# Attention in a hybrid kernel: from one head over all queries to chunks of 512 queries and groups of four heads, with the keys of all heads kept in SBUF

## What is computed

```python
    # 16 heads of 8 dimensions, L = 2048 tokens
    scores = jnp.einsum('bhqd,bhkd->bhqk', q, k) * scale
    scores = scores + alibi_bias(H, L)[None]      # -inf where the key is later than the query
    attn = jax.nn.softmax(scores, axis=-1)
    ctx = jnp.einsum('bhqk,bhkd->bhqd', attn, v)
    ctx = ctx.transpose(0, 2, 1, 3).reshape(B, L, E)
    return jnp.einsum('ble,fe->blf', ctx, w_out)
```

## Time and profile before

| | us |
|---|---|
| median of 3 runs (2050.13 to 2059.32) | 2055.5 |
| the profiled execution, its own time | 2052.21 |
| its span, first to last instruction | 2050.4 |
| what lies around the span | 1.8 |
| attention a0, first instruction to last addition to x | 514.8 to 993.7 |
| attention a1, the same | 1517.2 to 1990.7 |

### The profile page before, as it was taken

How to read it: one execution, slowest core, us unless ns; L and a number is a source line. 1 busy time by engine, 2 the same in 40 slices (tenths; PEclk the granted TensorE clock), 3 DMA queues, 4 the chain that set the end, 5 groups by cost and what they waited for, 6 DMA issues and landing times. The chain is left out here.

```text
span 2050.4 us, 47996 instructions
## 1 busy us (share of the span) xinstructions
PE 1835.4 (90%) x18588; PEld 979.6 (48%) x18588; DVE 1588.0 (77%) x3383; ACT 1175.0 (57%) x2361; POOL 553.9 (27%) x520
## 2 busy tenths in 40 slices
PE   6888888999799999998799978888769999999967
PEld 2444454444255555554544424444543555555454
DVE  6799965666889999983555568999668999999545
ACT  4676623222278888886222256765343888888815
POOL 3799930000200000000100037999230000000022
PEclk9899998999699999999799988999886999999969
DMA  5343300411302332211031022444012233322200
GB/s 158 102 139 123 134 1 1 83 52 31 110 25 54 52 52 57 52 26 22 2 83 52 31 62 95 127 123 118 1 58 66 51 56 58 59 57 42 30 5 21
DMA packets 68271, 126.88 MB, mean 62 GB/s; under 512 B 20919, under 2 KB 30676, under 8 KB 66572
## 3 DMA queue, kind: packets, MB, share of 16 engines
q1 hardware_dynamic: 67628, 123.27, 23.8%
q10 hardware_dynamic: 416, 0.54, 0.1%
HBM read 105.15 MB, written 16.84 MB: 59 GB/s over the span
## 5 line engine op out<-in xcount | busy, mean ns | idle before, releaser
L1757 ACT ACTIVATE a_probs<-a_ps_k 128x512 f32<-128x512 f32 (+3 forms) x1280 | 598.8, 546 | 225.0 <-PE a_ps_k L1671 128.7
L1653 PE MATMUL a_ps_q<-a_k_op,a_q_op 84*32 84x512 bf16 (+7 forms) x5120 | 537.1, 366 | 24.2 <-DMA a_k_op<-a_k_parts 9.0
L1817 DVE TENSOR_REDUCE a_maxes<-a_ps_q 128x1 f32<-128x512 f32 x768 | 504.2, 686 | 66.4 <-PE a_ps_q L1653 63.7
L1667 PE MATMUL a_ps_k<-a_q_op,a_k_op 87*32 87x512 bf16 (+7 forms) x5120 | 518.7, 353 | 2.4 <-ACT a_probs L1757 0.6
L1689 PE MATMUL a_ps_o<-a_probs,a_vh 128*32 128x512 f32 (+3 forms) x2752 | 318.4, 508 | 1.3 <-ACT a_probs L1757 0.8
L1653 PEld LDWEIGHTS a_ps_q<-a_k_op,a_q_op 72*32 72x32 bf16 (+1 forms) x5120 | 187.6, 97 | 170.4 <-DVE a_maxes L1817 69.0
L1814 DVE CUSTOM_DVE_ANT_0 a_ps_q<-a_ps_q,all_c_mask_q 128x128 f32<-128x128 f32 (+3 forms) x512 | 248.3, 496 | 5.4 <-PE a_ps_q L1653 4.3
L1667 PEld LDWEIGHTS a_ps_k<-a_q_op,a_k_op 75*32 75x32 bf16 (+1 forms) x5120 | 185.9, 96 | 135.6 <-ACT a_probs L1757 85.3
L1088 ACT ACTIVATE e_silu<-e_psg,all_me_b 128x512 f32<-128x512 f32 x128 | 87.7, 687 | 229.1 <-PE e_psg L1020 229.0
L1897 POOL CAST a_max_parts<-a_neg_max 128x16 bf16<-128x16 f32 x32 | 6.3, 196 | 750.5 <-DVE a_neg_max L1822 750.5
L1171 DVE SCALAR_TENSOR_TENSOR e_mid<-e_psv,all_me_b,e_silu 128x512 f32<-128x512 f32 x128 | 95.8, 750 | 128.8 <-PE e_psv L1022 125.0
(11 more groups left out here) (295 smaller groups left out, 2590.6 us busy)
## 6 DMA issues: line engine op xcount, KB each, us to landing
m0st_c_rows<-m_bc_rows SPq DMA_DIRECT2D x32, 512.0 KB
e_w_rows<-e_comb SPq DMA_DIRECT2D x64, 256.0 KB, 3.3
m1st_c_rows<-m_bc_rows SPq DMA_DIRECT2D x32, 512.0 KB
a_q_op<-a_q_parts SPq DMA_DIRECT2D x30, 288.0 KB
a_k_op<-a_k_parts SPq DMA_DIRECT2D x30, 288.0 KB
a_outputs<-a_o_sb SPq DMA_DIRECT2D x480, 18.0 KB
m0st_b_rows<-m_bc_rows SPq DMA_DIRECT2D x32, 256.0 KB
m1st_b_rows<-m_bc_rows SPq DMA_DIRECT2D x32, 256.0 KB
```

The source lines that it names most:

```text
L1653: last = pe.matmul(ps_q[32 * r:32 * r + 32, use % QB, 0:width], q_op[h % SLOT][0:NR, part(t, r)], k_op[h % SLOT][0:NR, kc * CH:kc * CH + w ...
L1667: last = pe.matmul(ps_k[32 * r:32 * r + 32, b % KB, 0:width], k_op[h % SLOT][:, part(j, r)], q_op[h % SLOT][:, c * CH + first:c * CH + fir ...
L1757: act.activation(probs[:, n % PSLOT, 0:width], ps_k[:, b % KB, 0:width], ACT.Exp).then_inc(exp_done, 1)
L1817: dve.tensor_reduce(found, bank, AX.X, ALU.max).then_inc(q_read, 1)
```

## The change

The work is regrouped. There are 16 steps: for each chunk of 512 queries, four groups of four heads. A step holds four heads' items of one chunk of queries, so steps have 16, 32, 48 and 64 items, four steps of each.

- The keys of all heads lie in SBUF, one operand buffer of 16 heads by 512 keys for each chunk (`k_op[c]`), loaded once. Chunk 0 is loaded by group of four heads on SP, chunks 1 to 3 on ACT's queue, each in one DMA of 72 rows by 8192 elements, once the chunk's parts are stored, and all of it stands in ACT's program ahead of the first exponential. Before it projects its third chunk, ACT waits until the first chunk's parts are stored, and so on (the parts have two buffers in place of four).
- The query operands have four slots by step (72 rows by 4 heads by 512).
- The order of the weights is changed so that dimensions come first and heads second; a chunk's rows then lie one behind the other in DRAM.
- The first form runs one step and 14 items ahead. Where the next step is longer, it issues items of the first form faster than one to one (2, 1.5 and 1.33 to one in steps 3, 7 and 11). In the last step there is none.
- The outputs of chunk c are loaded back, added, inverted, divided and projected while chunk c + 1 runs; `spread` and `output` use the banks of the first form. For c = 0 to 2 the addition of the partials is wholly on POOL. Only chunk 3 is left for the end.
- The values keep 9 columns a head (8 and a one) for all heads, in place of four slots of 32; POOL no longer copies them head by head. The banks are set to zero once.
- Stores take two heads in a DMA; the sums lie on 64 partitions by 128 in place of 128 by 64 (SB = 4).

```diff
+        k_last = m.sb("k_op3", [NR_MAX, HEADS * CH], BF16)
+        k_op = [m.sb(f"k_op{c}", [NR_MAX, HEADS * CH], BF16) for c in range(NC - 1)] + [k_last]
+        q_op = [m.sb(f"q_op{s}", [NR_MAX, HG * CH], BF16) for s in range(SLOT)]
+        vh = m.sb("vh", [P, NT * HEADS, DH + 1])
...
+        def position(b):
+            s, i = k_items[b][0], b - begin[k_items[b][0]]
+            after = size[s + 1] if s < LAST else size[s]
+            return min(begin[s + 1] + LEAD + -(-(i + 1) * after // size[s]), POSITIONS)
+        def event(c, n):
+            return position(begin[GROUPS * (c + 1)] + n)
+        prepare_at = {event(c, 24): c for c in range(NC - 1)}
+        spread_at = {event(c, 34): c for c in range(NC - 1)}
+        output_at = {event(c, 42): c for c in range(NC - 1)}
+        stats_at = {event(c, 46): c for c in range(NC - 1)}
+        normalise_at = {event(c, 60): c for c in range(NC - 1)}
...
+        def load_k(eng, c, first, n, sem):
+            rows = k_dram[c:c + 1, :, :, first:first + n, :].rearrange("o d b h t -> o (d b) (h t)")
+            eng.dma_start(k_op[c][0:PAIRS, first * CH:(first + n) * CH],
+                          rows.broadcast_to([SPL, SPL * DH, n * CH])).then_inc(sem, 16)
...
@@ PE
-            stream(turn, item, 0, NQ + LEAD)
+            first_forms(0, begin[1] + LEAD)
...
+            for b in range(NI):
+                if b + KB < NI:
+                    scores(b + KB)
+                first_forms(done, position(b))
+                done = position(b)
+                if b % 4 == 3:
+                    times_v(b - 3)
+            spread(NC - 1)
+            output(NC - 1)
@@ ACT
             for c in range(NC):
+                if c >= 2:
+                    act.wait_ge(stored[c - 2], STORED)
                 for o in range(2):
...
+            for c in range(1, NC):
+                act.wait_ge(stored[c], STORED)
+                if c == NC - 1:
+                    load_k_rows(act, c)
+                load_k(act, c, 0, HEADS, k_loaded[c])
             for b in range(AHEAD):
                 exps(b)
@@ POOL
+            for s in range(STEPS):
+                c = chunk_of(s) - 1
+                if c > 0 and s % GROUPS == 1:
+                    add_partials(c)
+                split_maxima(s)
+                if c >= 0 and s % GROUPS == 1:
+                    if c == 0:
+                        add_partials(c)
+                    ahead.power(pool, c)
@@ SP
+                for i, ready in enumerate((first_part, second_part, third_part)):
                     sp.wait_ge(ready[1], c + 1)
-                sp.dma_start(k_dram[:, :, :, chunk(c)].rearrange("h d s t -> (h d) s t"),
-                             parts[1][:, :, c, :]).then_inc(stored[c], 16)
+                    sp.dma_start(k_dram[c, :, i, :, :], parts[1][:, i, c % 2, :]).then_inc(stored[c], 16)
...
+            for c in range(NC - 1):
+                load_k_rows(sp, c)
+            store_parts(0)
+            sp.wait_ge(stored[0], STORED)
+            for i in range(GROUPS):
+                load_q(i)
+                load_k(sp, 0, HG * i, HG, k_first[i])
+                if i + 1 < NC:
+                    store_parts(i + 1)
             load_maxima(0)
```

More of the change, by code:

```diff
@@ L53 @@
 LORA = 32
-SB = P // HEADS
+SB = 4
 class Memory:
@@ L1583, in attention @@
[L1583 to L1594, removed]
+        QLOADS = 16 * (2 if alibi else 1)
+        KROWS = 16 * (2 if alibi else 1)
+        STORED = 16 * 2 * SPL
@@ L1656, in item, with spread @@
                 last.then_inc(q_ready, 1)
-            def scores(b):
-                h, n = divmod(b, NK)
-                c, j, first, width = k_items[n]
-                if n == 0:
-                    pe.wait_ge(max_loaded[h % SLOT], 16 * (h // SLOT + 1))
+            def spread(c):
+                use = spread_use[c]
+                pe.wait_ge(inverted, c + 1)
+                bank_free(use)
+                for j in range(SB):
+                    last = pe.matmul(ps_q[:, use % QB, j * JT:(j + 1) * JT], g["sel_head"][:, j, :], inv[:, :], start=True, stop=True)
+                last.then_inc(q_ready, 1)
@@ new lines, in output, with first_forms @@
+            def output(c):
+                use = output_use[c]
+                pe.wait_ge(q_read, spread_use[c] + 1)
+                bank_free(use)
+                for j in range(TPC):
+                    last = pe.matmul(ps_q[:, use % QB, tile(j)], total[:, tile(j)], w["wo"][:, :], start=True, stop=True)
+                last.then_inc(q_ready, 1)
+            def first_forms(begins, stops):
+                for p in range(begins, stops):
+                    if p in turn_at:
+                        turn(turn_at[p])
+                    if p in spread_at:
+                        spread(spread_at[p])
+                    if p in output_at:
+                        output(output_at[p])
+                    if p < NI:
+                        item(p)
@@ L1690, in times_v @@
                               start=j < 4, stop=j >= TPC * c, skip_group_check=True).then_inc(pv_done, 1)
[L1692 to L1695, removed]
-                for j in range(SB):
-                    last = pe.matmul(ps_s[:, j * JT:(j + 1) * JT], g["sel_head"][:, j, :], inv[:, :], start=True, stop=True)
-                last.then_inc(spread_ready, 1)
-            def output(c):
-                pe.wait_ge(normed, c + 1)
-                if c >= 2:
-                    pe.wait_ge(added, c - 1)
-                for j in range(TPC):
-                    last = pe.matmul(ps_y[:, c % 2, tile(j)], total[:, c % 2, tile(j)], w["wo"][:, :], start=True, stop=True)
-                last.then_inc(y_ready, 1)
@@ new lines, in _ @@
+            for c in range(NC - 1):
[7 more added lines that the diff above has]
+                    store_parts(i + 1)
+            load_maxima(0)
+            sp.wait_ge(stored[NC - 1], STORED)
+            for s in range(STEPS):
+                c = chunk_of(s)
+                if s:
+                    store(s - 1, 1)
+                if s and s + SLOT - 1 < STEPS:
+                    load_q(s + SLOT - 1)
+                if c == 0:
+                    load_maxima(s + 1)
+                if c and s % GROUPS == 0:
+                    load_outputs(c - 1, s - 1, 0, HEADS)
+                if c == NC - 1 and s % GROUPS:
+                    load_outputs(c, s - 1, head(s - 1, 0), HG)
+                if s < LAST:
+                    store(s, 0)
+                    if c:
+                        load_maxima(s + 1)
@@ L2023 @@
+            for hh in range(HG):
+                sp.wait_ge(o_read, HG * LAST + hh + 1)
+                if hh < HG - 1:
+                    move_sums(sp, hh)
+                move_outputs(sp, hh)
 MAMBA = ["in_T", "conv_w", "conv_b", "x_T", "dt_T", "dt_b", "a_log", "d", "out_T"]
```

542 lines of the change are left out of this document (256 added, 286 removed).

## The result

The changed kernel takes 2194.6 us, median of 4 runs (2193.1 to 2200.9), against 2055.0 of the kernel before on the same chip: ratio 1.0686, 95% interval 1.0654 to 1.0718. Slower, as forecast, but by 139.6 us instead of 59, and outside the range. The profiled execution has a span of 2191.0 us, 140.6 more than before.

A forecast was written before the change was run, and what follows sets the result against it. The kernel before was taken as PE bound with poor ends. First score 25.0 us later and the rest 4.6 longer made 29.6 us an attention, 59 for two: 2114 us, range 2050 to 2142.

The forecast's parts named there:

- Three engines, ACT's program as a gate: Beginning: each chunk's keys take 15.1 us on three engines at 78 GB/s; no exponential precedes the third load in ACT's program.
- The maxima land at 584 to 596 ... I take 587: Beginning: step 0's maxima wait behind group 3's 30 packets (4.7 us), plus up to 10 us for their own 16.
- The pitch of the steps: Stream: PE sets 8.95, 18.8, 29.6 and 40.3 us a step by chunk; DVE bounds steps 3, 7, 11 at 16.7, 26.3, 35.9.
- the prediction's own sign of being wrong: Stream: a step of chunk 3 that differs from 40.3 us by over 1 us would show the forecast wrong.
- the term for the clock: Stream: 4.3 us added because the second form began with 8 us at clock 0.53, which stays so.
- The spreads and outputs: 7.0: Stream: spreads and outputs of three chunks, 1.16 us each on PE, add 7.0 us to a stream PE bounds.
- DVE's own work for them fits into its slack, nearly; POOL's three additions have 15 us: Stream: DVE's 4.9 us a chunk for projections nearly fits its slack of 2 to 4 us a step.
- The end: After the last copy: only chunk 3 is left, a chain of 15 us in place of 21.3.
- 1: Key loads do no harm: first score at 554, 11 us earlier, 6.4 gained an attention, 2043 us; chance 0.16.
- 2: Key loads harm partly: first score at about 570 + 3, 8 later, 4.6 longer, 2080 us; chance 0.14.
- 4: Nothing measurable: earlier start and longer stream cancel, first score at 560, 2055 us; chance 0.08.
- Rival 3: PE stays at 1.2 GHz through chunk 0's steps: 27 us an attention on top, up to 2165; chance 0.10.

The follow-up runs named there:

- Experiment 2: Changed kernel with ACT's loads of keys of chunks 1 to 3 issued as four loads of four heads, rows of 4 KB instead of 16 KB: 2180.6 us.
- experiment 1: Changed kernel with every load of keys issued as three loads of 24 rows, one for each repeat of the block: 2123.3 us.
- experiment 6: Changed kernel with the two additions of the sums of chunks 0 to 2 moved from DVE to POOL: 2164.0 us.
- 4: Changed kernel with the sums and outputs of chunks 0 to 2 neither loaded, added, inverted nor projected, only chunk 3 at the end: 2154.9 us.
- experiment 5: Changed kernel with POOL's three additions of partial outputs of chunks 0 to 2 on 4 columns instead of 512: 2171.1 us.
- 3: Changed kernel with ACT's three key loads issued behind its first four exponentials and at the first score of chunks 1 and 2: 2157.4 us.
- 7: Changed kernel with keys in three loads of 24 rows, chunk 2's issued at the start of step 1, chunk 3's at step 6: 2126.0 us.

## Why the prediction was right in kind and wrong in size

- **Three engines, ACT's program as a gate**: right. The second and third loads of keys were forecast at 557 to 559 and at 581, and issued at 560.0 and 583.1; the share of 19%, 78 GB/s and clock 0.5 until the first score were there.
- **"The maxima land at 584 to 596 ... I take 587"**: this step failed, by 15 us in a0 and 24 in a1. They landed at 602. The term that was mis-sized is the queue ahead of them. I let group 3's 30 packets pass in 4.7 us, as if alone, and charged only the maxima's own 16 with a row of 16 KB each. By my own one-for-one reading of the earlier trace rows all 46 wait, an estimate of 46 x 0.63 = 29 us, and from the issue at 573.8 they took 28.5. That the two agree so well is in part luck: in these 28.5 us q10 moved 105 packets, 35 an engine over three engines or some 22 us at 0.63, the third load was issued only at 583.1, and q1 moved 322 packets, the parts of chunk 3 among them. What the trace does show is that the maxima land in the last microsecond of the third load. That SP's issues are held by the backlog as well (11.45 us for three) was in no row that I had. Experiment 2 shows that the rows' size is a part of it, 14 us, and experiment 1 that more engines give 38.
- **The pitch of the steps**: right where nothing else happens (29.6, 40.3 against 29.6, 40.8 and 39.9). The three steps bound by DVE were forecast too short by 6.0 us together, steps 4 and 6 by 3.3; no experiment asked why. The 53.6 us of step 12 are the prediction's own sign of being wrong, a step of chunk 3 more than 1 us from 40.3. By the earlier trace rows the term for the clock is 8 x 0.47 = 3.8 us and not 4.3, which changes nothing.
- **"The spreads and outputs: 7.0"**: right in size, 7.3 and 7.4 by experiment 6 against 4, with DVE's rest of the work in it.
- **"DVE's own work for them fits into its slack, nearly; POOL's three additions have 15 us"**: this step failed, by 14.5 us in a0 and 8.1 in a1 (B of the changed kernel less B of experiment 6), some 8 and 2 of them the clock of step 12. Total slack over a step was the wrong measure: PE is only three banks ahead of DVE, and a block of 3 us in DVE's program stops it. I also costed the additions at their time alone, though they run beside POOL's; experiment 5 shows that part, 1 us a projection. In a0 the clock fell behind such a stop, as it did in experiment 2 and did not in 3 and 7.
- **The end**: right, 13.5 for 15.
- **The rivals**: 1, 2 and 4 fell. Rival 3, PE at 1.2 GHz through all of chunk 0, did not happen (0.60 for 9 us); its time, 2165, was nearer than mine for another reason. By the Trainium skill, DMA: Bandwidth & Descriptors, section Bandwidth, I had estimated 3.5 us for each load; the third took 20 here, from its issue at 583.1 to 603.3. The page's figures are for transfers over 128 partitions issued by GpSimd, and this load has 3 as its slowest dimension.

## What to carry to other kernels

Read a load's slowest dimension before its bytes: a repeat of 3 in front made the largest transfers of the kernel run on three engines, and everything small behind them paid. When work goes into a stream that is full, the price of a block is not its share of an engine's slack but the time by which it outlasts the buffers between its engine and the bound one, and here each such addition was 1 us dearer beside another engine's additions. When one execution's step is 8 us longer, look at the same step in the other traces before giving the difference to the edit. Before a redesign for the sake of an idle end, try an order: two swapped lines in the kernel before gave 0.7%.

## What was not expected of the hardware

- A backlog in the DMA queues stretches the issuing itself: a store's issue on SP took 3.8 us (11.45 for three) instead of 0.6.
- A VectorE addition of 64x128 that takes 0.28 us alone took 1.25 to 1.30 beside POOL's additions, and one of POOL's grew from 1.28 to 1.46.
- One stop of 1.94 us of a PE that had been full was followed by 16 us at half clock in a0. In a1 the same step had 1.53 of 4 us busy and then a clock of 0.58 for 4 us only. In a0 of experiments 3 and 7 stops of 2.00 and 1.87 us were followed by no fall at all. What decides stays open.
